# Search counts in 16 bits, expert 0's remainders on VectorE, a longer TensorE run through the gather, first rows in halves

## What is computed

```python
x_flat = x.reshape(n, c)                      # n = 4096 rows, c = 256
scores = (x_flat @ Wg.T).T                    # 8 experts
top_vals, token_idx = jax.lax.top_k(scores, capacity)   # capacity = n / 8 = 512
token_w = jax.nn.softmax(top_vals, axis=-1)
xg = x_flat[token_idx]
h = silu(einsum('eic,ehc->eih', xg, W1)) * einsum('eic,ehc->eih', xg, W3)
y = einsum('eih,ech->eic', h, W2) * token_w[..., None]
out = zeros_like(x_flat).at[token_idx.reshape(-1)].add(y.reshape(-1, c))
```

## Time and profile before

| | |
|---|---|
| median of 3 runs | 873.8 us (873.3 to 874.51) |
| time of the profiled execution | 871.39 us |
| its span | 869.6 us |
| busy TensorE matmul / weight load | 674.4 / 516.8 us |
| busy VectorE / ScalarE / GpSimd | 676.0 / 496.4 / 215.7 us |
| chain that ended last, by engine | TensorE 45%, VectorE 22%, ScalarE 9%, GpSimd 6%, DMA 4% |

### The profile page before, as it was taken

The page is one execution under the profiler, slowest core; times in us unless marked ns, Lnnn a source line. Parts: engine busy times, 40 slices in busy tenths (PEclk is TensorE's granted clock), DMA queues, the critical chain, the costliest instruction groups (busy, mean ns, idle before and its releaser), DMA issues.

```text
span 869.6 us, 11451 instructions
## 1 busy us (share of the span) xinstructions
PE 674.4 (78%) x4007; PEld 516.8 (59%) x4007; DVE 676.0 (78%) x1334; ACT 496.4 (57%) x623; POOL 215.7 (25%) x175
## 2 busy tenths in 40 slices
PE   6872136999999727999999999969999993003998
PEld 5752124888888614465566656558887872003998
DVE  4997881787768278999778775897888999996554
ACT  1232010554334415686896887655658996995773
POOL 4445603166556442102210220003420000000000
PEclk9995555999999958999999999989999996555999
DMA  9927603345553570001013000003303631101242
GB/s 296 327 99 241 206 7 108 103 125 134 142 119 52 82 262 1 1 8 62 1 45 122 6 20 25 25 25 145 146 1 122 217 136 58 48 0 49 97 147 97
DMA packets 59491, 84.94 MB, mean 98 GB/s; under 512 B 7856, under 2 KB 47664, under 8 KB 57904
## 3 DMA queue, kind: packets, MB, share of 16 engines
q1 hardware_dynamic: 50176, 61.35, 21.0%
q0 software_dynamic: 7872, 21.11, 10.0%
q10 hardware_dynamic: 1392, 1.82, 0.6%
HBM read 53.73 MB, written 30.54 MB: 97 GB/s over the span
## 4 chain that ended last, share of the span: by engine, by line
PE 45%; DVE 22%; ACT 9%; POOL 6%; issue 6%; DMA 4%; DVEq 0%; ACTq 0%; POOLq 0%
PE bank L1903 8%; PE bank L1859 7%; PE bank L2092 4%; PE bank L1328 3%; PE bank L1362 3%; POOL x_dram L1950 3%; DVE peak L1632 3%; PE bank L1418 3%; PE bank L1385 3%; PE bank L1382 3%; PE bank L2104 3%; DVE above L772 2%; ACT wgateT L1794 2%; PE bank L1343 2%; DVE qx L1135 2%
## 5 line engine op out<-in xcount | busy, mean ns | idle before, releaser
L1224 ACT ACTIVATE x<-bank,bic 128x512 f32<-128x512 f32 x160 | 105.7, 692 | 38.0 <-PE bank L1362 36.4
L1135 DVE TENSOR_REDUCE qx<-bank 128x4 fp32r<-128x616 f32 x128 | 97.9, 796 | 23.0 <-PE bank L1328 21.4
L1859 PE MATMUL bank<-ux,uwh 128*128 128x512 f32 x384 | 98.8, 396 | 2.6 <-ACT ux L1760 2.4
L1859 PEld LDWEIGHTS bank<-ux,uwh 128*128 128x128 f32 x384 | 72.0, 190 | 20.8 <-issue 3.8
L1362 PE MATMUL bank<-qT,K 128*128 128x512 f32 x128 | 62.6, 499 | 4.3 <-ACT x L1224 2.0
L1328 PE MATMUL bank<-Kb,qTb 128*128 128x308 bf16 x256 | 54.9, 308 | 6.9 <-DVE qx L1135 2.7
L2054 ACT ACTIVATE wgateT<-bank 128x512 f32<-128x512 f32 x32 | 19.2, 599 | 71.3 <-PE bank L2092 71.3
L1849 PE MATMUL bank<-cst,amax 128*1 128x128 f32 x6 | 1.8, 354 | 69.9 <-DVE amax L1604 69.9
L2092 PE MATMUL bank<-xh,wh 128*128 128x512 f32 x128 | 51.1, 399 | 2.5 <-DVE xl L1973 2.5
L1859 PE MATMUL bank<-ux,uwl 128*128 128x512 f32 x192 | 52.3, 395 | 0.0
L2092 PE MATMUL bank<-xl,wh 128*128 128x512 f32 x128 | 51.1, 399 | 0.0
(11 more groups left out here) (353 smaller groups left out, 1996.6 us busy)
## 6 DMA issues: line engine op xcount, KB each, us to landing
xs_dram<-ux POOLq DMA_DIRECT2D x6, 1024.0 KB, 4.2
ux<-xs_dram POOLq DMA_DIRECT2D x6, 1024.0 KB, 5.7
x_dram<-x SPq DMA_DIRECT2D x4, 1024.0 KB, 5.2
xr<-in_w1T SPq DMA_DIRECT2D x8, 512.0 KB, 3.9
xr<-in_w3T SPq DMA_DIRECT2D x8, 512.0 KB, 4.8
xr<-in_w2T SPq DMA_DIRECT2D x8, 512.0 KB, 6.4
row_dram<-xn SPq DMA_DIRECT2D x8, 512.0 KB, 3.2
xr<-x_dram SPq DMA_DIRECT2D x8, 512.0 KB, 7.3
```

Of the source, the lines that this page charges most:

```text
L1135: dve.tensor_reduce(qx[:, k, g * GH:(g + 1) * GH, MROW].rearrange("p (u h) -> p u h", u=2), pair[i][:].rearrange("p (u x) -> p u x", u=2)[ ...
L1224: act.activation(pr[g % 2][h], S_[u % 2], ACT.Exp, bias=bic[:, s // 2, h // GH:h // GH + 1]).then_inc(p_done, 1)
L1859: mm = pe.matmul(bank[j][:, m * TB:(m + 1) * TB], w[:, c * HI + cols:c * HI + cols + P], x[:, part, c * TB:(c + 1) * TB], start=(w is uwh ...
```

## The change

1. **Counts in 16 bits.** `cnt3`, `cnt0` and `sums` become bf16 tiles, and the matrices `blk` and `tri` get bf16 copies `blk16` and `tri16`, made by GpSimd at the end of the first block. All 17 count matmuls and the two prefix matmuls use them. Counts are at most 256 and so exact in bf16.
2. **Remainders moved.** GpSimd no longer makes expert 0's three weight remainders in the search; VectorE makes them behind `idx`.
3. **Padding.** 24 padding matmuls in the place of 12; and 6 more (fp32r, 512 columns) between the transposes of expert 0's rows and its products.
4. **Halves.** Expert 0's rows are turned, rounded and subtracted in two halves of 512 columns, with a semaphore `e_half` from TensorE to ScalarE.

```diff
+        blk16, tri16 = sb(l0, "blk16", [P, P], BF16), sb(l0, "tri16", [P, P], BF16)
...
                     masked_keys(pool, raw0, Kb0, 0)
+                    pool.wait_ge(k_kb, NKB)
+                    pool.wait_ge(rest_in, 32)
+                    pool.tensor_copy(blk16[:], cst[:, C_BLK:C_BLK + P])
+                    pool.tensor_copy(tri16[:], cst[:, C_TRI:C_TRI + P])
...
-            cnt3 = sb(st, "cnt3", [P, 3])
+            cnt3, cnt0 = sb(st, "cnt3", [P, 3], BF16), sb(st, "cnt0", [P, 1], BF16)
-            sums, prior = sb(st, "sums", [P, 2]), sb(st, "prior", [P, 4])
+            sums, prior = sb(st, "sums", [P, 2], BF16), sb(st, "prior", [P, 4])
...
-                for m in range(3):
-                    pool.wait_ge(e_wh, m + 1)
-                    pool.tensor_tensor(wl0[:, m, :], w[0][:, m, :], wh0[:, m, :].bitcast(F32), ALU.subtract).then_inc(e_wl, 1)
...
-                pe.matmul(bank[1][:, 0:1], blk, cnt0, start=True, stop=True).then_inc(d_pe, 1)
+                pe.matmul(bank[1][:, 0:1], blk16[:], cnt0[:], start=True, stop=True).then_inc(d_pe, 1)
-                    pe.matmul(bank[1][:, 0:tests], blk, cnt3[:, 0:tests], start=True, stop=True).then_inc(d_pe, 1)
+                    pe.matmul(bank[1][:, 0:tests], blk16[:], cnt3[:, 0:tests], start=True, stop=True).then_inc(d_pe, 1)
-                pe.matmul(bank[3][:, 0:2], tri, sums[:], start=True, stop=True)
-                pe.matmul(bank[3][:, 2:4], blk, sums[:], start=True, stop=True).then_inc(d_sum, 1)
+                pe.matmul(bank[3][:, 0:2], tri16[:], sums[:], start=True, stop=True)
+                pe.matmul(bank[3][:, 2:4], blk16[:], sums[:], start=True, stop=True).then_inc(d_sum, 1)
...
-                for n in range(WARM):
-                    pe.matmul(bank[1][:, 0:512], hot_hi[:, n].rearrange("p h e -> p (h e)"),
+                for r in range(24):
+                    pe.matmul(bank[1][:, 0:512], hot_hi[:, r].rearrange("p h e -> p (h e)"),
...
-                    rows_lo(0, 0)
+                    for m in range(3):
+                        weights_lo(0, 0, m)
+                    for c in range(DC):
+                        dve.wait_ge(e_xh, c + 1)
+                        ins = dve.tensor_tensor(xl[0][:, c, :], bank[0][:, c * CAP:(c + 1) * CAP], xh[0][:, c, :].bitcast(F32), ALU.subtract)
+                    ins.then_inc(e_xl, 1)
...
-                    act.sem_inc(e_xh, 1)
-                    rows_hi(0, 0)
+                    for c in range(DC):
+                        act.wait_ge(e_half, c + 1)
+                        act.copy(xh[0][:, c, :], bank[0][:, c * CAP:(c + 1) * CAP]).then_inc(e_xh, 1)
...
-                    turned(0, 0)
+                    pe.wait_ge(e_got[0], 16 * CT)
+                    for c in range(DC):
+                        for k in range(CT):
+                            mm = pe.transpose(bank[0][:, c * CAP + k * P:c * CAP + (k + 1) * P], xg[0][:, k, c * P:(c + 1) * P], ident)
+                        mm.then_inc(e_half, 1)
+                    pe.sem_inc(e_xT, 1)
+                    for m in range(6):
+                        pe.matmul(bank[1][:, 0:CAP], wh0[:, m % 3, 0:P], wh0[:, m % 3, 0:CAP], start=True, stop=True)
```

More of the change, by code:

```diff
@@ L693, in build @@
         e_got = [sem(f"e_got{i}") for i in range(2)]
-        e_xT, e_xh, e_xl, e_h, e_gate, e_hT, e_hh, e_hl, e_y, e_yw, e_put, e_wh, e_wl = (
-            sem("e_" + n) for n in "xT xh xl h gate hT hh hl y yw put wh wl".split())
+        e_xT, e_xh, e_xl, e_h, e_gate, e_hT, e_hh, e_hl, e_y, e_yw, e_put, e_wh, e_wl, e_half = (
+            sem("e_" + n) for n in "xT xh xl h gate hT hh hl y yw put wh wl half".split())
         def gather(pool, e, dst):
@@ L731, in build @@
             ids = sb(st, "ids", [P, 2, 16, 4])
-            half, cnt0, want, cnt, rowmax, negmax, star, need, sume, rsum, bits, gone, before = (small[:, i:i + 1] for i in range(13))
+            half, want, cnt, rowmax, negmax, star, need, sume, rsum, bits, gone, before = (small[:, i:i + 1] for i in range(12))
             d_dve, d_cnt, d_pe, d_act, d_out = (sem(n) for n in ("d_dve", "d_cnt", "d_pe", "d_act", "d_out"))
@@ L739, in build @@
             TOK = bank[3][:, 512:512 + P].rearrange("p (q l e) -> p q l e", q=2, e=4)
-            WARM = 12
             MAXES, MAXROW, PRIOR, SLOTS, EXPS, WTS, IDS, SPREAD = range(1, 9)
@@ L758, in search_vector @@
                 ch, tot = Chain(dve, d_dve), Chain(dve, d_tot)
-                dve.tensor_scalar(junk[:], sg[:], 0.0, 0.0, ALU.is_ge, ALU.add, accum_out=cnt0).then_inc(d_cnt, 1)
+                dve.tensor_scalar(junk[:], sg[:], 0.0, 0.0, ALU.is_ge, ALU.add, accum_out=cnt0[:]).then_inc(d_cnt, 1)
                 dve.tensor_reduce(rowmax, sg[:], AX.X, ALU.max).then_inc(d_mid, 1)
@@ L895, in search_tensor @@
             def search_tensor(pe):
-                blk, tri = cst[:, C_BLK:C_BLK + P], cst[:, C_TRI:C_TRI + P]
+                blk = cst[:, C_BLK:C_BLK + P]
                 def halves(dst, src):
@@ L937, in search_tensor @@
                 mm.then_inc(d_sum, 1)
-                for n in range(WARM):
-                    pe.matmul(bank[1][:, 0:512], hot_hi[:, n].rearrange("p h e -> p (h e)"),
-                              hot_id[:, 8 * n % 48:8 * n % 48 + 8].rearrange("p r l e -> p (r l e)"), start=True, stop=True)
+                for r in range(24):
+                    pe.matmul(bank[1][:, 0:512], hot_hi[:, r].rearrange("p h e -> p (h e)"),
+                              hot_id[:, 8 * r % 56:8 * r % 56 + 8].rearrange("p r l e -> p (r l e)"), start=True, stop=True)
         l0.close()
```

## The result

The changed kernel takes 858.83 us (857.61 to 859.07, 4 runs), beside 873.55 us (871.83 to 874.51, 4 runs) for the kernel before. The ratio is 0.9831 with a 95% interval of 0.9812 to 0.9849: 14.7 us faster, where 14.75 were forecast. The forecast time was 859.0. Both kernels vary by some us from one execution to the next, and a later comparison with 9 more runs of the kernel before (median 870.81) and 4 of the changed one (858.72) gave 0.9857 (0.9839 to 0.9876), which is 12.1 us. So the size of the gain is known to about 2 us. That forecast and measurement agree to 0.2 us is luck. From there the same 14.75 us would give 856.1 to 856.5, and the changed kernel measured 858.83 and 858.72.

A forecast was written before the change was run, and what follows sets the result against it. Bound by one chain of waits through search, gather and expert 0's first products. 5.8 + 5.3 + 2.9 + 1.9 - 1.05 - 0.1 = 14.75 us off 873.8 gives 859.0; full range 857.0 to 862.8.

The forecast's parts named there:

- the prediction's own signs of being wrong: A digit above 2.4 us, clock 0.50 at expert 0's products, or gather's landing moved over 2 us against the list.
- Counts in 16 bits: Search: a 16-bit count takes 0.36 us less; over 17 counts 5.8 us gained, ends 3.8 and 6.8.
- The upper bound of the saving: Search counts: 0.42 us saved each, from the f32 tail of 0.05 behind a 16-bit load, 0.18 in all.
- Long digit: Search: the 7.90 us digit, waiting for GpSimd's subtractions, goes back to 2.60 us, 5.3 us gained.
- SyncE's loads: Search: rival that three weight loads issued then cause the long digit; 5.3 us stay, 864.3 us; chance 0.05.
- The gather behind the remainders: Behind the list: VectorE's remainders hold the gather's first two instructions, 1.05 us of delay, ends 0 and 2.9.
- The rival, all three remainders first: Behind the list: the gather waits for all three subtractions, 2.9 us of delay and not 1.05; 860.9 us; chance 0.08.
- Padding and the clock: Before expert 0's products: with 24 padding matmuls the clock holds, products take 10.99 us and not 13.87, 2.9 us gained.
- the rival: Around expert 0's rows: the clock falls again in the gap before the transposes, 2.4 us lost, 861.4 us; chance 0.35.
- Halves: From the rows' landing to expert 0's first product: 2.6 us in the place of 4.50, 1.9 us gained.
- what is gained here moves the end by as much: After expert 0: nothing behind the chain waits for a fixed time, so the whole gain reaches the end.

The follow-up runs named there:

- moved: Kernel before with only expert 0's three remainders moved from GpSimd's search to VectorE behind the list; ratio 0.9961, median 867.29 us.
- poolrem: Changed kernel with the three remainders put back on GpSimd inside the search; 861.79 us, ratio 0.9895 to the kernel before.
- again: Changed kernel run once more, unaltered, for its spread and a second profile; 858.72 us (857.22 to 860.38).
- pads33: Changed kernel with 33 padding matmuls ahead of the rows in the place of 24; 859.03 us.
- spread: Changed kernel with remainders spread: first in VectorE's wait for the list, second behind the list, third behind the rows; 857.65 us, ratio 0.9837.
- spread2: As the kernel spread, plus two reads of constants on VectorE delaying the second remainder until the gather's first instruction has begun; 856.08 us, ratio 0.9829.
- counts: Kernel before with only the counts in 16 bits and the two casts; ratio 0.9935, median 865.49 us.
- pads: Kernel before with only 24 padding matmuls ahead of the rows in the place of 12; ratio 1.0000, median 870.07 us.
- nofill: Changed kernel without the six padding matmuls behind the transposes; 859.03 us.
- spread2nf: As spread2, but without the six padding matmuls behind the transposes; 858.77 us, ratio 0.9851.
- halves: Kernel before with only expert 0's rows in two halves, 12 padding matmuls ahead, none behind the transposes; ratio 0.9989, median 869.63 us.
- pads12: Changed kernel with 12 padding matmuls ahead of the rows in the place of 24, the six behind kept; 858.73 us.

## Why the prediction was right

The direction was right, and so was the mechanism of each step, but for what keeps the clock up, where the sum credits the wrong padding. The sum was some 2 us too high: 14.75 us were forecast, and the four stretches of the table gained 13.4 in the first profile, the span 12.3. That the time was hit all the same is the luck told above, a slow sample of the kernel before. By the prediction's own signs of being wrong, two came true in part: four digits lie above 2.4 us (2.44 to 2.53), and the clock read 0.50 in the first 1.4 us of expert 0's products in the first profile. By its own steps:

**Counts in 16 bits.** Taken as 0.36 us each, measured 0.40. The search of the changed kernel is 6.2 us shorter than that of moved, where 5.8 were taken. The upper bound of the saving (0.42, from a record of 0.18 us) came nearest: the record measured 0.186, though with a load of 0.104 and not 0.129, and 0.08 behind it and not 0.05. The 64 columns of the list's matmul (0.241) were the worse guide; why its record is longer no run shows. Against the saving, some of VectorE's small steps last 0.2 to 0.3 us longer beside GpSimd's row instructions, a term that was not in the sum. The casts showed no cost: the search began at 66.44, as early as before.

**Long digit.** 5.3 taken; 5.1 in moved, 5.8 between poolrem and the changed kernel. That GpSimd's subtractions and not SyncE's loads held VectorE is shown by moved. The half clock of the search lies in slices 4 to 7 of the page, not 5 to 7; nothing hangs on it.

**The gather behind the remainders.** 1.05 taken, 1.23 measured: the first instruction was held 0.53 us, not 0.3, the second 0.75, near the 0.8 taken. The row that the prediction took for a DMA instruction beside a subtraction from PSUM (182.32) began just as that one ended; the row at 199.95 above is one, and the reading stands. The rival, all three remainders first, is out: the second DMA instruction began at 125.58 and the remainders ended at 126.46. The Trainium skill's page "SBUF — State Buffer" ("Who interferes with whom") left open who comes first; here GpSimd got in after the running one, and the VectorE instructions behind it were not slowed (3.50 us for three).

**Padding and the clock.** The step took it that the clock holds through the first products, for 2.9 us. In again it held and the products took 11.11, 2.6 less than before. In the first profile the rival came true in part: it fell and was back within 3.5 us, and 2.1 were gained. Between the rivals it is a matter of which execution one looks at. Of the six profiles with at least 24 padding matmuls and the six, five held it (again, poolrem, pads33, spread, spread2) and one lost it, the one with the longest pause ahead of the rows (2.18 us; 1.61 or less in the five). Of the four without the six (counts, pads, nofill, spread2nf) that had it at full when the rows landed, all lost it before or within the first products. My sum charged the whole 2.9 us to the 24. The traces do not bear this out: the products took 13.45 us in pads (the 24 alone) and 13.49 in halves, against 13.71; 12.51 with both (nofill); 11.11 to 11.63 with the six added; and 11.00 in pads12, which has the halves and the six but only the first 12. So in these profiles the term comes from the halves and the six, the six about half of it; the six with the rows in one piece were not tried. The 24 buy 0.9 us in the transposes, which ran at full clock in all nine profiles that have them, and in one of five with 12 (counts). That transposes don't count as TensorE work in the same way for the clock, as the Trainium skill says ("TensorE: Matmul & The Clock Gate", Part 4), fits nofill and pads, where the clock fell with only transposes near; no run here tested it apart from the pauses around them.

**Halves.** 1.9 taken; 1.24 in the first profile, 1.66 with the clock held. The chain at full clock is 2.84 and not 2.6 us: in again ScalarE began 0.70 us behind the landing, not 0.52, each of its halves took 0.59, not 0.55, and so VectorE's second half ended at 2.60 and not 2.35.

**What was missing.** The two profiles' four stretches sum to 13.4 and 14.4 us gained, and the medians say 12.1 in set 3 (12.4 to 12.5, if the first 858.83 us are set against the kernel before of sets 1 and 2). The rest goes in two places that the prediction called unaffected ("what is gained here moves the end by as much"). From expert 0's end to the last products the stretch was 628.5 us before and in again, 629.7 in the first profile. From the last products' start to the end it was 71.8 us in both first profiles, and 74.2 in again.

Over all 14 profiles of this document both stretches have a short and a long form. The first is 628.3 to 628.7 us in nine and 629.7 to 631.0 in five. In four of these five (changed, nofill, spread2, spread2nf) the granted clock falls to 0.50 for 3.5 to 4 us at expert 3's transposes, in the last three at expert 5's too; in the nine it stays at full there; and all four have one more fall near 283 us. The fifth, counts, shows none of these, and its cause is open. The 576 last products take 68.2 to 68.4 us in nine, 69.6 in counts and 70.7 to 70.8 in four (nofill, pads33, spread, again). Why is open: in changed and again alike the granted clock is 1.00 from some 7 us behind their start on. Of the nine kernels that join the faster counts with other parts of the change seven have at least one long form; of the other five (before, counts, moved, pads, halves) one has. So the profiles hint that the changed kernel falls on the long side more often, which would be the missing 2 us. With one execution each they do not show it, and no run tests why.

## What to carry to other kernels

A tiny instruction that sits on the path and lasts two microseconds has a neighbour: look at what the other engine does in that time and whether their ends coincide, as VectorE's and GpSimd's did here. Moving that work moves its hold-ups too: beside an indirect DMA, start VectorE's two-input instructions just behind the DMA instruction and not just ahead of it. Padding for TensorE's clock is of most use in the last pause ahead of the real work: there it shortened the 48 products by 0.9 to 1.4 us in the profiles, while ahead of the data alone it brought nothing that the times show. And a gain early in a kernel need not reach its end in full: compare the later stretches too, in more than one execution.

## What the runs showed that was not expected

- A lone f32 count of three columns takes 0.60 us at 1.2 GHz, the same in bf16 0.20, a third of it.
- Beside GpSimd instructions with one tensor input VectorE's small steps last 0.2 to 0.3 us longer (0.44 and 0.48 instead of 0.16); beside those with two inputs, 2.34 us each, they last up to 2.34. Taking the latter away (moved) brought the steps back; taking the former away was not tried.
- An indirect DMA instruction of GpSimd is held by a running VectorE subtraction only if that runs when it starts: 1.75 us in spread, 1.22 us in spread2, for the same work 0.6 us apart.
- The last products (576 matmuls) took about 68.4 us in one execution and 70.8 in another of the same kernel, at full granted clock for all but the first 7 us in both.
- The clock can fall in the loop over the experts in one execution and hold in the next, after the same pause of 1.9 us, for about 1 us each time.
